# Masked queries of an attention stage: one VectorE addition and one GpSimd masking, or two fused VectorE operations

## The reference

```python
q = proj(layernorm(x), Wq, bq); k = proj(ctx, Wk, bk); v = proj(ctx, Wv, bv)   # proj: x @ W + bias
scores = einsum('bhqd,bhkd->bhqk', q, k) / sqrt(16)
scores = scores + where(query_block == key_block, 0, -65504)
x = x + (softmax(scores) @ v) @ Wo + bo
logits = layernorm(x) @ gate_w.T + expert_bias     # top 2 of 8 experts
x = x + layernorm(sum_e weight_e * (gelu(x @ up_e.T) @ down_e.T)) + layernorm(x)
```

## Time and profile before

| | |
|---|---|
| median of three runs | 822.94 us |
| the profiled execution | 824.23 us, span 822.4 us |
| TensorE busy | 720.0 us, 88% of the span |
| VectorE busy | 536.5 us, 65% |
| ScalarE busy | 363.5 us, 44% |
| GpSimd busy | 441.4 us, 54% |
| L1005, the masking on GpSimd | 32 of 1.04 us |
| L1013, `w_lo` on GpSimd | 32 of 2.13 us |

### The profile page before, as it was taken

One profiled execution on the slowest core, in us unless ns is written; L12 is line 12 of the kernel. 1 busy time (PEld: TensorE's weight loads), 2 busy tenths in 40 slices (PEclk: granted clock), 3 DMA queues, 4 the chain that ended last, 5 costly groups with the idle time before them and its releaser, 6 DMA issues.

```text
span 822.4 us, 20968 instructions
## 1 busy us (share of the span) xinstructions
PE 720.0 (88%) x6400; PEld 648.0 (79%) x6401; DVE 536.5 (65%) x1182; ACT 363.5 (44%) x657; POOL 441.4 (54%) x584
## 2 busy tenths in 40 slices
PE   4999999999999718599999999999999999999200
PEld 4999999999999514498899999998899898998100
DVE  4889888888888579455555555555555555554295
ACT  2877777777777403122222222222222222222184
POOL 3777787788787407524444444344443444422287
PEclk9999999999999855699999999999999999999655
DMA  4333333333332100111111111111111111110594
GB/s 157 109 108 121 104 121 103 120 104 119 103 121 85 41 7 0 54 38 53 53 51 47 44 49 45 45 51 51 51 51 45 45 51 45 45 38 27 171 304 164
DMA packets 39875, 64.54 MB, mean 78 GB/s; under 512 B 5408, under 2 KB 30240, under 8 KB 39840
## 3 DMA queue, kind: packets, MB, share of 16 engines
q1 hardware_dynamic: 31632, 42.37, 16.0%
q0 software_dynamic: 7488, 20.46, 7.7%
q10 hardware_dynamic: 720, 1.26, 0.5%
HBM read 45.46 MB, written 18.61 MB: 78 GB/s over the span
## 4 chain that ended last, share of the span: by engine, by line
PE 87%; DVE 4%; issue 3%; DMA 2%; POOL 2%; ACT 1%; SPq 0%; ACTq 0%; DVEq 0%; POOLq 0%
PE ps_a L530 25%; PE ps_b L544 25%; PE ps_b L433 7%; PE ps_a L391 4%; PE ps_b L400 4%; PE ps_c L412 4%; PE ps_c L417 3%; PE ps_a L468 3%; PE ps_a L455 2%; PE ps_c L498 2%; PE ps_c L514 2%; PE ps_a L479 1%; PE ps_c L378 1%; PE ps_a L443 1%; DMA w_hi<-y_rows 1%
## 5 line engine op out<-in xcount | busy, mean ns | idle before, releaser
L530 PE MATMUL ps_a<-area,w_hi 128*128 128x256 f16 x1248 | 207.7, 274 | 1.7 <-DVE area L795 1.7
L544 PE MATMUL ps_b<-w_hi,area 128*128 x1248 | 206.4, 273 | 0.0
L1055 POOL DMA_INDIRECT y_rows<-area x78 | 77.9, 999 | 209.4 <-ACT area L940 197.5
L530 PE MATMUL ps_a<-area,w_lo 128*128 128x256 f16 x624 | 170.7, 274 | 0.0
L544 PE MATMUL ps_b<-w_lo,area 128*128 x624 | 170.1, 273 | 0.0
L935 ACT ACTIVATE area<-ps_a 128x512 f32<-128x512 f32 x156 | 93.1, 597 | 142.0 <-PE ps_a L530 142.0
L530 PEld LDWEIGHTS ps_a<-area,w_hi 128*128 x1248 | 122.3, 98 | 16.1 <-issue 2.1
L544 PEld LDWEIGHTS ps_b<-w_hi,area 128*128 128x128 f16 x1248 | 122.1, 98 | 14.1
L793 DVE TENSOR_SCALAR area<-ps_c 128x512 f16<-128x512 f32 x39 | 27.0, 691 | 151.7 <-PE ps_c L514 151.7
L805 DVE SCALAR_TENSOR_TENSOR area<-area 128x512 f16<-128x512 f32 x156 | 108.3, 694 | 5.4
L940 ACT ACTIVATE area<-ps_b 128x512 f32<-128x512 f32 x39 | 23.3, 597 | 181.1 <-PE ps_b L544 181.1
(11 more groups left out here) (129 smaller groups left out, 1250.2 us busy)
## 6 DMA issues: line engine op xcount, KB each, us to landing
area<-weights SPq DMA_DIRECT2D x32, 512.0 KB, 3.3
w_hi<-y_rows SPq DMA_DIRECT2D x32, 256.0 KB, 4.0
resid<-x_in SPq DMA_DIRECT2D x32, 128.0 KB, 2.1
area<-ctx_t SPq DMA_DIRECT2D x32, 128.0 KB, 2.1
xn_rows<-area SPq DMA_DIRECT2D x32, 128.0 KB, 1.7
out<-w_lo SPq DMA_DIRECT2D x16, 256.0 KB, 2.6
area<-xn_rows,area POOLq DMA_INDIRECT x78, 2.8
y_rows<-area POOLq DMA_INDIRECT x78
```

Source lines behind the costliest of these rows:

```text
L530: mm = pe.matmul(ps_h[:, q, (ic % 2) * SLOTS:(ic % 2 + 1) * SLOTS], w[:, bass.ds(first + (hc * I + ic * P), P)], r[b][:, hc, :], start=(n ...
L544: mm = pe.matmul(ps_y[:, b, v * D:(v + 1) * D], g[b][:, ic, v * P:(v + 1) * P], w[:, bass.ds(first + (EXPERT_COLS + ic * D), D)], start=(n ...
L1055: pool.indirect_dma_start(y_rows[:, :], bass.IndirectOffsetOnAxis(ap=didx[b][:, v:v + 1], axis=0), y_s[b][:, v * D:(v + 1) * D], None).the ...
```

## The change

The masked queries are (ps_q + bias) x mask, for the two masks of even and odd heads. Before, VectorE adds the bias and GpSimd multiplies with both masks. After, VectorE writes `q_m` in two fused operations straight from PSUM, one for each mask h: ps_q x mask_h + (bias x mask_h), where bias x mask_h (`bq_m`) is worked out once ahead of the loop, in four small operations. The tile `q_b` and the semaphore `qb_r` are gone, and `q_r` counts two for each tile. Both buffers, ps_q and `q_m`, are now held and released by VectorE alone.

```diff
-        q_b = carve(HC * P).rearrange("p (c n) -> p c n", c=HC)
+        bq_m = carve(2 * HC * NB).rearrange("p (h y) -> p h y", h=2)
...
                 if valid(t):                                   # TensorE, scores
-                    pe.wait_ge(q_r, t + 1)
+                    pe.wait_ge(q_r, 2 * (t + 1))
...
                     pe.wait_ge(xt_r, t + 1)                    # TensorE, query projection
-                    since(pe, qb_r, t)
+                    since(pe, q_r, 2 * t)
...
                     dve.wait_ge(k_ps, t + 1)                   # VectorE
-                    since(dve, q_r, t)
-                    dve.tensor_tensor(q_b, ps_q, bq_s.unsqueeze(2).to_broadcast([P, HC, P]), ALU.add).then_inc(qb_r, 1)
+                    for h in range(2):
+                        dve.scalar_tensor_tensor(q_m.rearrange("p c b h q -> p (c b) h q")[:, :, h, :],
+                                                 ps_q.rearrange("p c (b q) -> p (c b) q", b=NB), cst[:, C_MASK + h:C_MASK + h + 1],
+                                                 bq_m[:, h, :].unsqueeze(2).to_broadcast([P, HC * NB, BLOCK]),
+                                                 ALU.mult, ALU.add).then_inc(q_r, 1)
...
             dve.wait_ge(small_in, 16)
+            for h in range(2):
+                for c in range(HC):
+                    dve.tensor_scalar(bq_m[:, h, c * NB:(c + 1) * NB], bq_s[:, c:c + 1].to_broadcast([P, NB]),
+                                      cst[:, C_MASK + h:C_MASK + h + 1], None, ALU.mult).then_inc(bq_r, 1)
+            dve.wait_ge(bq_r, 2 * HC)
...
-                t, half, b = here(j, u, 1)                     # GpSimd
-                if valid(t):
-                    if isinstance(t, int) and t == 0:
-                        pool.wait_ge(small_in, 16)
-                    pool.wait_ge(qb_r, t + 1)
-                    since(pool, s_ps, t)
-                    pool.tensor_tensor(q_m.rearrange("p c b h q -> p (c b) h q"),
-                                       q_b.rearrange("p c (b q) -> p (c b) q", b=NB).unsqueeze(2).to_broadcast([P, HC * NB, 2, BLOCK]),
-                                       cst[:, C_MASK:C_MASK + 2].unsqueeze(1).unsqueeze(3).to_broadcast([P, HC * NB, 2, BLOCK]),
-                                       ALU.mult).then_inc(q_r, 1)
```

More of the change, by code:

```diff
@@ L220, in program @@
             sem(n) for n in ("wv_scaled", "wv_hi_r", "wv_lo_r", "ctx_scaled", "ctx_hi_r", "ctx_lo_r"))
-        q_r, qb_r, k_ps, k_r, v_ps, v_r = (sem(n) for n in ("q_r", "qb_r", "k_ps", "k_r", "v_ps", "v_r"))
+        q_r, bq_r, k_ps, k_r, v_ps, v_r = (sem(n) for n in ("q_r", "bq_r", "k_ps", "k_r", "v_ps", "v_r"))
         s_ps, max_r, sub_r, p_r, pt_ps, pt_r = (sem(n) for n in ("s_ps", "max_r", "sub_r", "p_r", "pt_ps", "pt_r"))
```

## The result

| | before | after |
|---|---|---|
| median | 822.52 us (4 runs) | 870.12 us (4 runs, 869.55 to 871.51) |
| span of the profiled execution | 822.4 us | 868.5 us |
| TensorE / VectorE / GpSimd busy | 720.0 / 536.5 / 441.4 us | 735.8 / 594.2 / 411.0 us |

The changed kernel is slower by 47.6 us: the ratio is 1.058, with a 95% interval of 1.056 to 1.060.

The account below looks back on a forecast made before the run. Prediction: TensorE bounds the attention stage; `w_lo` ahead of xn2 lengthens 24 steps by 1.54 us, 37 us in all, so 824.23 + 37 = 861.2 for the profiled execution, median 860; likeliest case 852 to 868, 8 in 10 830 to 870.

Parts of the forecast that it names:

- TensorE sets the pace, the masking is off the path: Attention stage: TensorE busy all 33 us of a window; nothing waits for GpSimd's masking, so moving it gains nothing.
- The added operation: VectorE's two fused operations for one addition: 0.46 us more a step, hidden by itself in a 0.82 us wait.
- The removed wait: GpSimd without the masking's wait: `w_lo` follows `ctx_lo`, gets in ahead of L651, which ends at 6.97 us.
- The order: At the end of `ctx_lo`, waiting L642 passes before `w_lo`; the other order would give 9.94 us a step, 42 in all.
- A step of 9.75 us: Attention loop: VectorE's own queue sets a step of 9.75 us instead of 8.21, 1.54 more.
- the sum: Attention loop: 24 steps x 1.54 = 37 us, with 0 to 2 us for the first five steps.
- rival 4: Attention stage: dearer, 875 us or more, as TensorE's clock could fall from 2.4 to 1.2 GHz in places; chance 0.03.
- Rivals 1 and 2: `w_lo` and L651: first, no meeting, 823 us, chance 0.12; second, only each pass's first step, 832 us, 0.07.
- Rival 3: Attention stage: faster, 815 us, if scores or weights' pipeline hung on GpSimd, saving 8 us; chance 0.02.

Follow-up runs that it names:

- e1_gap: Changed kernel with one wait more: GpSimd starts `w_lo` only when VectorE has written xn2; 823.80 us.
- e5: Changed kernel with eight more TensorE transposes a step ahead of the wait for xn2, and the load of x issued ahead of the store of xn2; 861.34 us.
- e6: Kernel before with `w_lo` ahead of the masking on GpSimd, plus the added transposes and earlier load of x of e5; 858.17 us.
- e8: Changed kernel with only the load of x issued ahead of the store of xn2 on SyncE; 871.35 us.
- e3_half: Changed kernel with `w_lo` in two halves of 512 columns, the second moved to the end of GpSimd's step; 838.80 us.
- e2_swap: Kernel before, arithmetic unchanged, with `w_lo` moved ahead of the masking on GpSimd; 870.50 us.
- e7: Changed kernel with xn2 written by a scalar_tensor_tensor with the root in PSUM, in place of a tensor_scalar within SBUF; 826.53 us.

## Why the prediction was right in kind and wrong in size

- **TensorE sets the pace, the masking is off the path: right.** e1_gap has the whole change and costs nothing that can be told (0.8 us, with 1 inside the interval).
- **The added operation, 0.46 us a step, hidden by itself: right.** Its two instructions have a mean of 0.471 us. It is hidden in e1_gap, and costs 0.18 a step in e5 against e6.
- **The removed wait lets `w_lo` follow `ctx_lo` and get in ahead of xn2: right.** The order was the one I took: L642 passes first (0.7 to 0.8 us), then `w_lo`, then L651. My reason, the order of asking, is not shown by it: the start on record of `w_lo` lies between 0.12 us ahead of L651's and 0.01 behind it, and L651 stood still each time. Even in my own L642's start is 0.01 ahead of L998's, and it was L642 that waited. That the two engines take turns when both have work would give the same order. It happened in 24 steps in a row, from the last step ahead of the loop on; I had put it one later at both ends.
- **A step of 9.75 us: right.** It is 9.69 to 9.78 in 13 steps of the changed kernel, and 24 steps take 234.2 us in e5. There is a little luck in this sum: most steps of e5 take 9.72, and the first of each pass 9.9 to 10.1.
- **The step that failed is the sum: I took all 24 at that pace, and TensorE's clock for unchanged.** That it could fall "in places" stood as rival 4 with 0.03. It fell in seven places, for 10.3 us by e5 and e8, and the 10.0 us for which L588 waits for TensorE in the changed kernel agree. What is left of its 24 steps is 245.9 - 244.5 = 1.4 us against e8. The load of x behind the late store, which was not on my list at all, is the likely cause, but this is not shown: the waits for x on record come to 0.6 us, and e8 as a whole is no faster than the changed kernel.
- **The reason against rival 4 was a misread row.** I took the clock of 1.00 in the window 0 to 20 us as a sign that TensorE could be half idle at full clock. But the time of its matrix products says otherwise. The same eight records of L412 in the timeline before, early and in the loop:

```profile
9.12 2.05 PE L412 MATMUL ps_c<-area 128*128 128x128 f32 x8 [1.93 <-ACT area L858]
...
146.14 1.06 PE L412 MATMUL ps_c<-area 128*128 128x128 f32 x8
```

TensorE ran at about half its later pace there, and the first record of its clock in that trace begins at 20.9 us. The 1.00 ahead of it was no measurement. The trace after confirms this reading. There the clock is on record earlier, and in a stretch at 0.50 the same eight records take nearly as long (a window and a row of the timeline):

```profile
15.20:18.20 3.00, 3.00 (x23) 2.78 (x20) 1.37 (x2) 2.63 (x5) 2.40 (x5) 0.50 0.00 0
...
16.68 1.95 PE L412 MATMUL ps_c<-area 128*128 128x128 f32 x8
```

The trace before also had windows in which a TensorE with gaps did lose its clock, at the end of the attention stage and in routing:

```profile
262.00:290.00 28.00, 21.08 (x158) 18.35 (x156) 16.23 (x48) 13.70 (x28) 13.63 (x19) 0.89 0.13 42
290.00:345.00 55.00, 27.86 (x117) 15.99 (x118) 39.39 (x70) 9.96 (x14) 22.84 (x20) 0.53 0.06 16
```

With these rows read rightly, a TensorE that goes from fully busy to busy for 8.2 of 9.75 us would have been worth more than a chance of 0.03.

Rivals 1 and 2 fell with the trace after: `w_lo` met L651 in 24 steps in a row, and in none of them did it come too late. Rival 3 fell with e1_gap, where the moved work brings nothing. Still open is what exactly of TensorE's idle time makes the clock fall: e3_half idles less (busy for 31.17 of 33 us from 126 to 159) and has one stretch, e2_swap six, the changed kernel seven.

## What to carry to other kernels

An instruction that waits can be a spacer: before one is taken off a GpSimd queue, look at what then moves up, and which VectorE operation stands beside it in the new place. A tensor_scalar within SBUF stood still for the whole of a GpSimd operation here (0.40 to 2.2 us), and one wait put elsewhere (e1_gap) or one input moved to PSUM (e7) undid nearly all of it. When a step gets longer on another engine, price TensorE's new idle time at the slow clock too, by how long like matrix products take in stretches where it was partly idle. The clock column alone can mislead ahead of its first record.

## What the runs showed of the hardware

- A tensor_scalar of VectorE within SBUF and a GpSimd operation did not run at the same time, and the turn passed between them even where an engine's instructions follow without a gap. L642 waited for L1006 and went ahead of `w_lo`; `w_lo` went ahead of L651, in 24 of 24 steps. Whether the order of asking decides or the engines alternate is open.
- The same arithmetic as a scalar_tensor_tensor with one input in PSUM took 0.48 us beside the same GpSimd operation (e7), where the tensor_scalar took 2.2.
- TensorE with 28.77 us of work in 33 lost its full clock in places, although none of its waits in the loop was longer than about 2 us; eight more transposes a step, 1.04 us, kept the clock up in the steps that had them, and the program was 4.9 us faster.
